# Condition network ahead of the first convolution, and mixing weights computed by batch in 32x32 tiles

## What is computed

```python
# block 0
y = conv1d(x, weight[32, 8, 9], groups=4, padding=4) + (cond @ c_weight.T)[:, :, None] + bias[None, :, None]
x = x + quantised_matmul(y, ffn0_weight)        # rows of y and of the weight rounded to int8, rescaled, to fp16
# block 1
h = gelu(cond @ W0 + b0); h = gelu(h @ W1 + b1)
att = softmax(h @ W2 + b2)                       # 64 x 8: each batch's shares of 8 mixing matrices
agg_w = einsum('bk,koi->boi', att, weight[8, 32, 32]); agg_b = att @ bias_k
z = einsum('boi,bih->boh', agg_w, x) + agg_b[:, :, None]
x = x + scale * (z @ (2 * kernel - 1))           # kernel is boolean, 512 x 512
```

## Time and profile before

| | |
|---|---|
| median of three runs | 126.05 us (125.63 to 126.14) |
| profiled execution, its own time | 127.2 us |
| its span, first to last instruction | 125.2 us |
| TensorE matmuls | 114.5 us busy, 91% of the span, 1759 |
| TensorE weight loads (beside the matmuls) | 77.2 us |
| VectorE / ScalarE / GpSimd | 76.0 / 41.9 / 70.6 us busy |
| bytes moved by DMA | 18.60 MB, mean 149 GB/s |
| mean granted TensorE clock | 0.944 of full speed |

### The profile page before, as it was taken

How to read it: one execution, slowest core, us unless ns; L and a number is a source line. 1 busy time by engine, 2 the same in 40 slices (tenths; PEclk the granted TensorE clock), 3 DMA queues, 4 the chain that set the end, 5 groups by cost and what they waited for, 6 DMA issues and landing times.

```text
span 125.2 us, 4314 instructions
## 1 busy us (share of the span) xinstructions
PE 114.5 (91%) x1759; PEld 77.2 (62%) x1759; DVE 76.0 (61%) x189; ACT 41.9 (33%) x81; POOL 70.6 (56%) x102
## 2 busy tenths in 40 slices
PE   4978999998998894999999999999999998699990
PEld 1345545653665562677768667777777684587880
DVE  6270578825965990078819855982987278275532
ACT  0414154355357402524083126406331722420210
POOL 6970047557974776007852882677088407975640
PEclk9999559589999999599999999999999999999999
DMA  1898999995999988309394731505132251021024
GB/s 42 220 200 304 222 232 216 205 220 124 228 225 224 228 178 242 73 14 284 105 260 135 216 118 58 168 5 169 67 109 93 80 163 56 32 84 63 25 99 153
DMA packets 11378, 18.60 MB, mean 149 GB/s; under 512 B 1624, under 2 KB 2776, under 8 KB 11360
## 3 DMA queue, kind: packets, MB, share of 16 engines
q1 hardware_dynamic: 10512, 17.84, 54.0%
q10 hardware_dynamic: 560, 0.44, 1.9%
q0 software_dynamic: 288, 0.06, 0.4%
HBM read 14.12 MB, written 4.19 MB: 146 GB/s over the span
## 4 chain that ended last, share of the span: by engine, by line
PE 77%; DVE 6%; DMA 5%; issue 4%; ACTq 2%; POOL 2%; ACT 2%; POOLq 0%; DVEq 0%
PE ps L361 21%; PE ps L404 13%; PE ps L407 11%; PE ps L396 11%; PE ps L389 10%; DMA xs<-in_x_dram 5%; PE ps L381 4%; DVE q_max L554 2%; PE ps L338 2%; DVE mix L599 1%; PE ps L321 1%; ACT xq L765 1%; POOL x L875 1%; PE ps L313 1%; PE ps L423 1%
## 5 line engine op out<-in xcount | busy, mean ns | idle before, releaser
L875 POOL TENSOR_TENSOR x<-xr,delta 128x512 f32<-128x512 f32 x16 | 18.7, 1168 | 29.8 <-DVE delta L636 29.1
L361 PE MATMUL ps<-xs,conv_st 32*32 32x256 f32 x1280 | 31.5, 424 | 3.2 <-issue 1.8
L361 PEld LDWEIGHTS ps<-xs,conv_st 32*32 32x32 f32 x1280 | 17.3, 106 | 10.9 <-issue 5.4
L881 POOL TENSOR_TENSOR z_lo<-z,z_hi 128x512 fp32r<-128x512 f32 x16 | 20.4, 1277 | 4.7 <-ACT z_hi L771 3.7
L606 DVE TENSOR_REDUCE row_max<-ysb 128x2 f32<-128x512 f32 x16 | 10.8, 678 | 18.3 <-ACT ysb L759 18.3
L771 ACT ACTIVATE z_hi<-z 128x512 fp32r<-128x512 f32 x16 | 10.1, 631 | 32.5 <-DVE z L644 32.3
L404 PE MATMUL ps<-sign,z_hi 128*128 128x512 f32 x60 | 18.3, 428 | 0.4 <-ACT aggb_bc L752 0.4
L396 PEld LDWEIGHTS ps<-mix,x 128*128 128x128 f32 x128 | 16.6, 191 | 2.8 <-POOL x L875 0.6
L389 PE MATMUL ps<-wq,xq 128*128 128x512 f16 x64 | 16.6, 381 | 0.9 <-DVE delta L636 0.5
L396 PE MATMUL ps<-mix,x 128*128 128x128 f32 x128 | 17.1, 276 | 0.1
L759 ACT ACTIVATE ysb<-ps,bias_col 128x256 f32<-128x256 f32 x32 | 13.3, 479 | 10.4 <-PE ps L361 10.3
(11 more groups left out here) (108 smaller groups left out, 100.3 us busy)
## 6 DMA issues: line engine op xcount, KB each, us to landing
xs<-in_x_dram SPq DMA_DIRECT2D x31, 256.0 KB, 5.1
xr<-in_x_dram SPq DMA_DIRECT2D x16, 256.0 KB, 3.9
out_dram<-res SPq DMA_DIRECT2D x15, 256.0 KB, 2.0
q_raw<-in_L_ffn_weight_dram SPq DMA_DIRECT2D x4, 256.0 KB, 3.5
xs<-in_x_dram ACTq DMA_DIRECT2D x1, 256.0 KB, 6.3
sign_raw<-in_L_ffn_kernel_dram SPq DMA_DIRECT2D x1, 256.0 KB, 8.0
out_dram<-res SPq DMA_DIRECT2D x2, 128.0 KB, 1.7
w_sb<-in_L_cond_W_dram ACTq DMA_DIRECT2D x2, 64.0 KB, 4.8
```

Source lines behind the costliest of these rows:

```text
L361: mm = pe.matmul(Y[r][C * j:C * (j + 1), HL * qs[0]:HL * (qs[-1] + 1)], conv_st[C * r:C * (r + 1), m].rearrange("k o p -> k (o p)"), xs[C ...
L875: nc.gpsimd.tensor_tensor(x1[:, t % NX1, :], xr[:, t % 4, :], delta[:, t % 2, :], ALU.add)\
L881: nc.gpsimd.tensor_tensor(z_lo[:, t % NH, :], z[:, t % 2, :], z_hi[:, t % NH, :].bitcast(F32), ALU.subtract)\
```

## The change

TensorE's prologue: the second layer, the condition's bias and the logits stand ahead of the wait for `x`; the first pair's convolution follows in one piece, broken only by `attention` ahead of its last step. The fillers change from (11, 6, 2) to (8, 1, 1, 2, 1), all of them ahead of the wait for `x`. The mixing weights are computed by batch position `b` within a tile: 32 matmuls for each of four `b`, each with weights of 8 x 32 (`mixk[:, o, :]`) and 16 moving columns (the 16 batches of that `b`), all 32 in the one 32x32 tile of the array at row 0 and column 32b. The result stands on the partitions where `mix` wants it, so that one copy of 32 x 512 for each `b` fills it: `b` = 0 and 1 on ScalarE, 2 and 3 on VectorE. `agg_sb` and GpSimd's copies are gone. VectorE takes the softmax ahead of the convolution's bias and of the weight's maxima. `fside_row`, `w2_sb` and `b2_rows` move from GpSimd's queue to ScalarE's, and ScalarE's load of `x` moves to SyncE, whose list of loads puts tiles 4 and 5 ahead of the plain rows and of the signs.

```diff
-    WARM = (11, 6, 2)
+    WARM = (8, 1, 1, 2, 1)
...
-        def mix_block(b, ol):
-            return mix[C * b:C * (b + 1), :, C * b + ol:C * (b + 1):OL]
-        def agg_block(b, ol, src=FIN):
-            return src[C * ol:C * (ol + 1), :].rearrange("p (o t b) -> p b t o", o=OH, b=NB)[:, b]
+        def mix_block(b):
+            return mix[C * b:C * (b + 1), :, C * b:C * (b + 1)]
+        def agg_block(b):
+            return FIN[C * b:C * (b + 1), :].rearrange("p (o t) -> p t o", t=NT)
...
@@ sync @@
             load_x(1, 0)
+            load_x(1, 1)
...
+            load_x(4, 0)
+            sp.wait_ge(x_in[0][1][0], 32)
+            load_x(4, 1)
+            load_x(5, 0)
+            sp.wait_ge(x_in[0][1][1], 32)
+            load_x(5, 1)
             load_rows(0)
+            load_rows(1)
...
@@ tensor @@
-            def mixing_weights(hs):
-                for h in hs:
-                    mm = pe.matmul(FIN[:, B * h:B * (h + 1)],
-                                   mixk[:, OL * h:OL * (h + 1), :].rearrange("k o c -> k (o c)"), att_T[:],
-                                   start=True, stop=True)
+            def mixing_weights(b):
+                for o in range(C):
+                    mm = pe.matmul(FIN[C * b:C * (b + 1), NT * o:NT * (o + 1)], mixk[:, o, :], att_T[:, b:B:NB],
+                                   start=True, stop=True, tile_position=(0, C * b))
+                mm.then_inc(agg_mm, 1)
...
+            warm(WARM[1], Y[0])
             pe.wait_ge(cond_copied, 1)
             hidden1()
+            warm(WARM[2], Y[0])
...
-            warm(WARM[1], Y[0])
-            pe.wait_ge(conv_copied, 2 * SH)
-            conv_inputs(0, [0])
-            conv_step(0, [0], 0)
+            warm(WARM[3], Y[0])
             hidden2()
-            conv_step(0, [0], 1)
+            warm(WARM[4], Y[0])
...
@@ vector @@
+            softmax_first()
             conv_bias()
+            softmax_second()
...
@@ scalar @@
-            act.wait_ge(pads_set, 2)
-            load_shift(act, 1, 1)
+            act.dma_start(fside_row[:], fside.rearrange("(a c) -> a c", a=1)).then_inc(fside_in, 16)
+            act.dma_start(w2_sb[:], w2).then_inc(w2_in, 16)
+            act.dma_start(b2_rows[:], b2.partition_broadcast(B)).then_inc(b2_in, 16)
...
@@ gpsimd @@
-            for ol in range(2):
-                for b in range(NB):
-                    need(pool, agg_spread, NB * ol + b)
-                    nc.gpsimd.tensor_copy(mix_block(b, ol), agg_block(b, ol, agg_sb)).then_inc(agg_spread, 1)
-            pool.wait_ge(agg_spread, 2 * NB)
             first_sum(0)
-            signs(0)
             first_sum(1)
-            signs(1)
             quantise(2)
             quantise(3)
+            signs(0)
+            signs(1)
```

More of the change, by code:

```diff
@@ L455, in _ @@
             mm.then_inc(ctx_ready, 1)
-            conv_step(0, [0], 2)
             logits()
-            conv_step(0, [0], 3)
-            conv_step(0, [0], 4).then_inc(conv_done, 1)
+            pe.wait_ge(conv_copied, 2 * SH)
+            conv_inputs(0, [0])
+            for m in range(MS - 1):
+                conv_step(0, [0], m)
+            attention()
+            conv_step(0, [0], MS - 1).then_inc(conv_done, 1)
+            mixing_bias()
+            pe.wait_ge(bias_copied, NB)
+            mixing_weights(0)
+            mixing_weights(1)
             pe.wait_ge(ident_h_ready, 2)
@@ L462, in _ @@
             ffn0_weights(1)
-            attention()
-            pe.wait_ge(bias_copied, NB)
-            warm(WARM[2], FIN)
-            mixing_bias()
-            mixing_weights(range(0, 4))
+            mixing_weights(2)
+            mixing_weights(3)
+            ffn0_weights(2)
+            ffn0_weights(3)
+            ffn0_scales()
             conv_inputs(0, [1])
             conv_step(0, [1], 0)
-            mixing_weights(range(4, OH))
-            ffn0_weights(2)
-            conv_step(0, [1], 1)
-            ffn0_weights(3)
-            ffn0_scales()
-            conv_step(0, [1], 2)
             pe.wait_ge(wq_ready, LC)
             turn_tile(0)
+            conv_step(0, [1], 1)
+            conv_step(0, [1], 2)
+            turn_tile(1)
             conv_step(0, [1], 3)
-            turn_tile(1)
+            conv_step(0, [1], 4).then_inc(conv_done, 1)
             ffn0_tile(0)
-            conv_step(0, [1], 4).then_inc(conv_done, 1)
             ffn0_tile(1)
@@ L593, in mixed_bias, with mixing_weights @@
                    .then_inc(aggb_lo, 1)
-            def mixing_weights(ol):
+            def mixing_weights(b):
                 dve.wait_ge(mix_zeroed, 1)
-                dve.wait_ge(agg_mm, 1)
-                for b in range(NB):
-                    last = dve.tensor_copy(mix_block(b, ol), agg_block(b, ol))
-                last.then_inc(agg_copied, 1)
+                dve.wait_ge(agg_mm, b + 1)
+                dve.tensor_copy(mix_block(b), agg_block(b)).then_inc(agg_copied, 1)
             def maxima(t):
@@ L890, in _ @@
             quantise(1)
-            pool.wait_ge(mix_zeroed, 1)
-            pool.wait_ge(agg_in, 1)
-            pool.wait_ge(quant_done, 2)
-            for ol in range(2):
-                for b in range(NB):
-                    need(pool, agg_spread, NB * ol + b)
-                    nc.gpsimd.tensor_copy(mix_block(b, ol), agg_block(b, ol, agg_sb)).then_inc(agg_spread, 1)
-            pool.wait_ge(agg_spread, 2 * NB)
             first_sum(0)
-            signs(0)
             first_sum(1)
-            signs(1)
             quantise(2)
             quantise(3)
+            signs(0)
+            signs(1)
             for t in range(4, NT + 5):
```

49 lines of the change are left out of this document (16 added, 33 removed).

## The result

The changed kernel takes **136.78 us**, the median of four runs (135.53 to 137.65), against 126.05 before: ratio 1.0825 with a 95% interval of 1.0745 to 1.0906. It is slower, as forecast, but by more than twice as much: the forecast was 130.8 and its range ended at 136.0. The profiled execution has a span of 135.7 us and an own time of 137.65, against 127.2 before: +10.5.

What follows compares the result with a forecast made beforehand. TensorE was taken to bound the prologue: +1.2 - 5.67 + 8.2 + 2.0 - 1.0 = +4.7 us at the loop's start, nothing later, giving 130.8 us against a median of 126.05; range 124.0 to 136.0.

Steps and rivals of the forecast that it cites:

- The frame: Prologue from x's landing to the loop is a sum over TensorE; the change moves the loop's start, plus a possible stop shift.
- What leaves the path: After x lands, second layer, bias, logits, fillers with a wait, and old mixing weights leave TensorE's path: -5.67 us.
- What stands in front: Bias and logits ahead of the first convolution delay it from 9.88 to 11.1 us: +1.2, bounds +0.5 to +2.4.
- The price of a pair: New mixing: each weight load and matmul takes 32 ns, a quarter of the old 129; 256 pairs cost 8.2 us.
- the second term of the sum: The clock's surcharge on the mixing pairs: +2.0 us if a quarter run at 1.2 GHz, 8.2 if all do.
- rival 3: All mixing pairs, and the pieces behind them, run at 1.2 GHz: +11.9 us, time 138, chance 0.11.
- The share at 1.2 GHz: In the new mixing stretch, a quarter of the 256 pairs runs at the low clock: +2.0 us.
- The credit of the clock: Prologue pieces that ran at 1.2 GHz before may run at 2.4: about 2 us possible, -1.0 taken.
- The stop: TensorE's 1.84 us halt at 47.05 us, read as late instructions; could vanish or come earlier and longer; some 3.3 us.
- rivals 2 and 4: The forecast without the stop at 47 us, 127.5 (0.18); late instructions in the prologue, about 134.5 (0.10).
- Nothing-terms: Copies, GpSimd's new order, ScalarE's extra issues, the moved queues and reordered loads: hidden behind other work, all at nothing.
- The rival that the network isn't ready in time: Before the convolution, small loads land with x, so the network isn't done: up to +1.2 us, inside the forecast's share.

Runs made afterwards that it cites:

- e1: The changed kernel with the old mixing weights and copies, all else of the change kept: 125.26 us, ratio 0.9896.
- e2: The kernel before with only the new mixing weights and copies: 136.54 us, ratio 1.0807.
- e7: The changed kernel with each new mixing matmul streaming 32 columns instead of 16, still in one tile: 137.6 us.
- e10: The changed kernel with the second pair's convolution steps 0, 1 and 2 between the four groups of new mixing matmuls: 139.04 us, ratio 1.0971.
- e8: e1 with the queues and SyncE's order of loads from the kernel before: 125.26 us, ratio 0.9962.
- e3: The changed kernel with the same 128 mixing matmuls reordered so that four 32x32 tiles take turns: 132.55 us.
- e16: e1 with the first ffn0_tile ahead of the second pair's last convolution step, and SyncE waiting ahead of each load from x10 on: 123.81 us.
- e6: The kernel before with 64 tiny matmuls added where TensorE waits for x: 129.02 us, ratio 1.0259.

## Why the prediction was right or wrong, step by step

**The frame was right.** (One reading of the rows was not quite: the DMA line of the earlier trace rows has a five in its tenth slice, and no term uses it.) The difference stands at the loop's start (+12.6), and what is after it changes only through the stop (-2.1). e1 and e2 show that it belongs to the mixing weights, as the sum said: the only large positive term.

**What leaves the path**: -5.67 stands; the pieces are gone from TensorE between the first convolution and the loop.

**What stands in front**: forecast +1.2, measured 12.68 - 9.88 = +2.8. Three things went the dear way. The weight of the second layer (`w_sb` in the trace) landed at 8.91, and that layer took 0.66 us from 9.05, which I hadn't put ahead of the bias at all. A filler of 0.43 us stands between the two, so that the bias began at 10.14 and not at 9.4. And the four pieces of the bias took 0.45 to 0.62 us, nearly all at 1.2 GHz's price. That passes my bound of +2.4 by 0.4.

**The price of a pair**: forecast 32 ns at 2.4 GHz, measured 32. The number came out, but partly by luck: the rule behind it, that a quarter of the columns on both sides costs a quarter, no run shows. e7 shows that at 1.2 GHz doubling the columns adds 6 ns of 53, which isn't in proportion. Nor does the price double at 1.2 GHz, as the second term of the sum and rival 3 took it: it goes from 32 to 53.

**The share at 1.2 GHz**: this is the step that failed. I let a quarter of the pairs run there (+2.0); it was all but some 47 of 256. The 256 took 0.80 + 5.10 + 6.75 = 12.65 us, of which 256 x 32 ns = 8.2 is the price at 2.4 GHz, as forecast, and 4.4 the clock's (forecast 2.0, +2.4). With the stop of 1.19 the stretch is 13.84 against 10.2, **+3.6** on the forecast. The prediction's own words, "longer and just as thin", pointed to nearly all pairs, and rival 3 was this case; it got 0.11. The quarter had no row behind it.

**The credit of the clock** (-1.0): this failed with it, wrong in sign. What isn't mixing, from the first convolution to the loop, took 44.62 - 12.68 - 13.84 = 18.1 us, against 22.13 - 5.67 = 16.5 before: +1.6 instead of -1.0. Four convolution steps took 4.46 us where 2.4 GHz would need 2.8, L317 took 1.81 instead of 1.56, and the second `ffn0_tile` waited 0.99 for `delta`. I had credited a dense stretch with keeping its clock; in e10 dense steps behind thin work run at the low clock as well (granted clock 0.50 from 20.8 to 37.8 us, 1.18 us for 22 or 23 of the 32 pairs of a step that takes 0.69 in all at 2.4 GHz).

**The stop**: rightly read as the fetch of instructions (the transfers above show it), rightly said to vanish from 47 us or come earlier. It did both: -2.1 there, +1.19 in the mixing (rivals 2 and 4 in one), and the sum had neither.

1.6 + 3.6 + 2.6 is, unrounded, 7.9 of miss at the loop's start, less 2.1 behind it: 5.8, and 136.78 - 130.8 = 6.0. Rival 3 came within 1.2 us of the time (138), though with 16.4 us for pairs that took 12.65. **The range** ended at 136.0 because rival 3 was left outside; three terms depend on one clock, and I bounded them one by one, as if they could not all go wrong together.

**Nothing-terms**: the queues (e8) cost nothing, as said. GpSimd's new order was not tried alone; e1, which has it apart from the copies, is no slower than before. The rival that the network isn't ready in time was half true, within the 2.8.

## What to carry to other kernels

- Before replacing a few wide matmuls by many small ones, count pairs, and price them at the low clock, together with the dense work behind them; if they must be small, let neighbouring ones address different tiles (14 ns a pair instead of 52 at 1.2 GHz here).
- A stop of TensorE inside a run of matmuls, with no wait on record and the DMA full, may be its own instruction list. Count instructions from one stop to the next, look for a transfer of the instruction queue that ends shortly before TensorE goes on, and spread the loads that fill the DMA; moving them in a bunch moves the stop.
- Uncertain terms that hang on one cause (here the clock) belong into one rival with their sum, and its chance taken from the row that shows the cause at work.

## What the runs showed of the hardware that I had not expected

- Four 32x32 tiles that share rows and differ in columns work side by side: a pair starts every 8.5 ns at 2.4 GHz and every 13.9 at 1.2 (e3), a quarter of the 32 and 52 in one tile (means). With 32 columns instead of 16 one tile takes 60 ns at either clock (e7).
- TensorE outruns the supply of its own instructions: 256 of them in 3.2 us, and then a stop of 2.91 us (e3). It goes on 1.2 to 1.8 us after the 16 KB transfer has ended, in all 28 such stops. The Trainium skill (Runtime: NRT & Kernel Launch, Instruction fetch mechanics) calls the cost of crossing a block of 16 KiB mostly hidden. Where the DMA has air the rows agree (no stop in e16 from 30 to 78 us); behind stretches where it is full they don't (0.3 to 2.9 us).
- 1.68 us of tiny matmuls in idle time cost 3 us (e6). By its profile the clock is the way: 0.50 granted from 11.8 to 28.8 us.
